# Flamingo block with two gated layers on one core: q and k of the second attention stacked in both halves of the partitions, its small matmuls as pairs of 64-row tiles

## What is computed

```python
def _L1_xattn_ref(query, key, value, Wq, Wk, Wv, Wo):   # DIM 512, 32 heads of 16, 8 key-value heads
    q = (query @ Wq).reshape(b, sq, 32, 16).transpose(0, 2, 1, 3)
    k = (key @ Wk).reshape(b, sk, 8, 16).transpose(0, 2, 1, 3)     # each serves 4 heads
    v = (value @ Wv).reshape(b, sk, 8, 16).transpose(0, 2, 1, 3)
    scores = jnp.einsum('bhqd,bhkd->bhqk', q, k) * 16 ** (-0.5)
    probs = jax.nn.softmax(scores, axis=-1)
    out = jnp.einsum('bhqk,bhkd->bhqd', probs, v)
    return out.transpose(0, 2, 1, 3).reshape(b, sq, DIM) @ Wo
x = x + jnp.tanh(g_xattn[1]) * _L1_xattn_ref(_layernorm(x), ctx_4096, ctx_4096, ...)
```

## Time and profile before

| | us |
|---|---|
| median of 3 runs | 1134.33 (1128.93 to 1134.96) |
| profiled execution, its own time | 1125.34 |
| its span, first to last instruction | 1123.5 |
| TensorE (PE) busy | 1012.8 |
| VectorE (DVE) busy | 665.8 |
| ScalarE (ACT) busy | 482.3 |
| GpSimd (POOL) busy | 376.5 |
| mean granted TensorE clock | 0.967 |

### The profile page before, as it was taken

The page is one execution under the profiler, slowest core; times in us unless marked ns, Lnnn a source line. Parts: engine busy times, 40 slices in busy tenths (PEclk is TensorE's granted clock), DMA queues, the critical chain, the costliest instruction groups (busy, mean ns, idle before and its releaser), DMA issues. The chain is left out here.

```text
span 1123.5 us, 18617 instructions
## 1 busy us (share of the span) xinstructions
PE 1012.8 (90%) x6780; PEld 877.3 (78%) x6780; DVE 665.8 (59%) x1128; ACT 482.3 (43%) x938; POOL 376.5 (34%) x251
## 2 busy tenths in 40 slices
PE   2989999999999999999999999998898579999964
PEld 1979889898898898989889898897776357777543
DVE  5467467457556646745745674673486546667396
ACT  2356336436535634643643563372131125555311
POOL 4306503711730640361173065032892300000054
PEclk9989999999999999999999999999998689999986
DMA  5001100100200110110020011000531173121000
GB/s 172 35 1 57 39 1 27 67 0 0 93 0 0 56 37 0 47 46 0 0 93 0 0 56 56 0 1 1 171 102 38 38 205 63 29 56 29 1 1 37
DMA packets 29617, 46.49 MB, mean 41 GB/s; under 512 B 3216, under 2 KB 12048, under 8 KB 29584
## 3 DMA queue, kind: packets, MB, share of 16 engines
q1 hardware_dynamic: 29008, 46.03, 13.5%
q10 hardware_dynamic: 576, 0.00, 0.0%
HBM read 41.83 MB, written 4.19 MB: 41 GB/s over the span
## 5 line engine op out<-in xcount | busy, mean ns | idle before, releaser
L446 DVE TENSOR_TENSOR ptL<-tbank,ptH 128x512 fp32r<-128x512 f32 x192 | 132.3, 689 | 84.5 <-ACT ptH L330 84.5
L330 ACT ACTIVATE ptH<-tbank 128x512 fp32r<-128x512 f32 x192 | 115.9, 604 | 109.2 <-PE tbank L554 108.9
L281 POOL TENSOR_TENSOR oTL<-o_norm,oTH 128x512 fp32r<-128x512 f32 x32 | 41.3, 1291 | 347.1 <-ACT oTH L350 347.1
L554 PE MATMUL tbank<-ident,probs 128*128 128x128 f32 x864 | 132.2, 276 | 16.6 <-DVE ptL L446 12.3
L459 DVE TENSOR_REDUCE negmax<-score 128x1 f32<-128x768 f32 x128 | 119.5, 949 | 19.5 <-PE score L74 19.5
L417 DVE TENSOR_REDUCE sumsq<-probs 128x2 f32<-128x256 f32 (+1 forms) x80 | 42.1, 526 | 142.3 <-ACT probs L325 71.8
L356 ACT ACTIVATE probs<-score,negmax 128x768 f32<-128x768 f32 x128 | 115.7, 904 | 15.4 <-DVE negmax L459 15.4
L72 PE MATMUL obank<-ptH,vH 128*128 128x256 f32 x384 | 121.8, 317 | 0.0
L554 PEld LDWEIGHTS tbank<-ident,probs 128*128 128x128 f32 x864 | 97.9, 140 | 26.9 <-DVE ptL L446 15.1
L276 POOL TENSOR_TENSOR rnorm<-sumsq,neg_half 128x2 f32<-128x2 f32 (+1 forms) x80 | 71.9, 901 | 111.3 <-DVE sumsq L419 111.3
L73 PE MATMUL score<-wkvL,kvT_hi 128*128 128x256 f32 x384 | 108.7, 283 | 0.0
(11 more groups left out here) (250 smaller groups left out, 2467.9 us busy)
## 6 DMA issues: line engine op xcount, KB each, us to landing
wqo_stage<-in_wq SPq DMA_DIRECT2D x9, 1024.0 KB, 5.7
wqo_stage<-in_wo SPq DMA_DIRECT2D x8, 1024.0 KB, 5.3
wkv_stage<-in_wkv SPq DMA_DIRECT2D x9, 512.0 KB, 6.5
a_qS<-q_scratch SPq DMA_DIRECT2D x32, 128.0 KB, 3.8
ctx_stage<-in_ctxT SPq DMA_DIRECT2D x2, 1024.0 KB, 14.0
kS<-k_scratch SPq DMA_DIRECT2D x32, 64.0 KB, 2.1
q_scratch<-part SPq DMA_DIRECT2D x8, 256.0 KB, 4.0
wqo_stage<-in_down_w SPq DMA_DIRECT2D x3, 512.0 KB, 4.8
```

The lines of the kernel that those rows point to most:

```text
L330: act.activation(out, tbank[c % 2][:], ACT.Copy, scale=scale).then_inc(t_hi, 1)
L446: i = dve.tensor_tensor(out, tbank[c % 2][:], f32(hi), ALU.subtract)
L554: i = pe.transpose(tbank[c % 2][:, n * P:(n + 1) * P], block_in, S.ident[:])
```

## The change

`qS` and `kS` hold the same 64-row stack twice, in partitions 0 to 63 and in 64 to 127, so `load_k` and `load_q` issue 8 DMAs each in place of 4 (`STACK` doubles with them), and both memsets to zero and the waits for them go. Every matmul of the scores pass, of the transposed scores and of the maxima takes 64 rows: of two neighbours one reads the low half and the other the high half, and they write different banks. The negative maxima of a unit are now 8 matmuls of 128 columns in two groups of four (`add_maxima`): in the first group (`begin_maxima`) the low rows add their 64 queries to bank 0 and the high rows theirs to bank 1, in the second (`finish_maxima`) the banks are exchanged. The second group is issued one turn later, behind `scores_T` of the next unit, and it is what now releases the exp (`pe_sT`). `negmax` has 4 buffers in place of 2. `times_v` moves to `v % 4 == 2`, the transposes to `v % 4 == 3`, and `finish_quad` to `v % 4 == 0` of the quad after that.

```diff
-            sp.wait_ge(k_zeroed, 1)
             for s in range(2):
                 S.load_k(sp, s, s)
...
-            pool.memset(f32(S.kS[64:P, :, :]), 0.0).then_inc(k_zeroed, 1)
-            pool.wait_ge(k_zeroed, 1)
...
-    negmax = sb("a_negmax", [P, 4], f32r)
+    MB = 4
+    negmax = sb("a_negmax", [P, 2 * MB], f32r)
...
-    STACK = 8 * 16
+    STACK = 16 * 16
+    H = P // 2
+    low, high = slice(0, H), slice(H, P)
...
-            sp.wait_ge(zeroed, 2)
-
             def load_q(g, s):
-                for n in range(4):
-                    heads = q_dram[n // 2].rearrange("(h d) n -> d h n", d=D1)
+                for n in range(8):
+                    heads = q_dram[n // 2 % 2].rearrange("(h d) n -> d h n", d=D1)
...
-            pool.memset(f32(qS[64:P, :, :, :]), 0.0).then_inc(zeroed, 1)
-            pool.wait_ge(zeroed, 2)
...
-                    if v % GRP == 3 and (not first or v >= GRP):
-                        finish_quad(i, r - 1, v // GRP - 1)
+                    if v % GRP == 0 and (not first or v >= 2 * GRP):
+                        finish_quad(i, r - 2, v // GRP - 2)
...
-            finish_quad(TURNS - 1, QUADS * TURNS - 1, QUADS - 1)
+            for w in (QUADS - 2, QUADS - 1):
+                finish_quad(TURNS - 1, QUADS * (TURNS - 1) + w, w)
...
-                    q = b * SQ + t * P
-                    pe.matmul(score[t][:], qS[:, s, j, q:q + P], kS[:, s, b * SC:(b + 1) * SC],
+                    q, rows = b * SQ + t * P, (low, high)[t]
+                    pe.matmul(score[t][:], qS[rows, s, j, q:q + P], kS[rows, s, b * SC:(b + 1) * SC],
                               start=True, stop=True).then_inc(pe_s, 1)
+
+            def add_maxima(v, order, stop):
+
+                for t in range(2):
+                    m = negmax[:, 2 * (v % MB) + t:2 * (v % MB) + t + 1]
+                    for half, rows in enumerate((low, high)):
+                        bank = scoreT[v % 2][:, 512 * order[half]:512 * (order[half] + 1)]
+                        q = t * P + H * half
+                        x = pe.matmul(bank.rearrange("p (k q) -> p k q", k=2)[:, :, q:q + H],
+                                      m[rows].to_broadcast([H, P]), ident_r[rows, rows].unsqueeze(1).to_broadcast([H, 2, H]),
+                                      start=False, stop=stop and t == 1)
+                return x
 
             def scores_T(n, v, first):
 
                 s, b, j = unit(v)
                 if not first or v >= 2:
                     pe.wait_ge(s_exp, n - 1)
+                for k in range(2):
+                    for half, rows in enumerate((low, high)):
+                        key = b * SC + (2 * half + k) * P
+                        pe.matmul(scoreT[v % 2][:, 512 * half + k * SQ:512 * half + (k + 1) * SQ], kS[rows, s, key:key + P],
+                                  qS[rows, s, j, b * SQ:(b + 1) * SQ], start=k == 0, stop=False)
+
+            def begin_maxima(n, v):
+
                 pe.wait_ge(s_max, 2 * n + 2)
...
-                x.then_inc(pe_sT, 1)
+                add_maxima(v, (0, 1), False).then_inc(pe_m, 1)
+
+            def finish_maxima(n, v):
+
+                pe.wait_ge(pe_m, n + 1)
+                add_maxima(v, (1, 0), True).then_inc(pe_sT, 1)
...
                     scores_T(n, v, first)
+                    if not first or v >= 1:
+                        finish_maxima(n - 1, (v - 1) % NU)
+                    begin_maxima(n, v)
                     if not first or v >= GRP:
-                        if v % GRP == 1:
+                        if v % GRP == 2:
                             times_v(r - 1, (v // GRP - 1) % QUADS, i if v >= GRP else i - 1, first)
-                        if v % GRP == 2:
+                        if v % GRP == 3:
                             transpose_o(r - 1, (v // GRP - 1) % 2)
...
             def load_k(sp, g, s):
 
-                for n in range(4):
+                for n in range(8):
```

More of the change, by code:

```diff
@@ L696, in ffn0 @@
     pe_v, v_done = sem("pe_v"), sem("v_rows_done")
-    k_zeroed, stats3_done = sem("k_zeroed"), sem("stats3_done")
+    stats3_done = sem("stats3_done")
     w_in = {n: sem(f"{n}_in") for n in ("gate", "affine")}
@@ L1251, in attn1 @@
     win = sem("a_win")
-    pe_s, s_max, ident_set = sem("a_pe_s"), sem("a_s_max"), sem("a_ident_set")
+    pe_s, pe_m, s_max, ident_set = sem("a_pe_s"), sem("a_pe_m"), sem("a_s_max"), sem("a_ident_set")
     pe_sT, s_exp, pe_pv = (sem(f"a_{n}") for n in ("pe_sT", "s_exp", "pe_pv"))
@@ L1375, in maxima @@
                     dve.wait_ge(pe_s, 2 * n + t + 1)
-                    dve.tensor_reduce(negmax[:, 2 * (v % 2) + t:2 * (v % 2) + t + 1], score[t][:], AX.X, ALU.max,
+                    dve.tensor_reduce(negmax[:, 2 * (v % MB) + t:2 * (v % MB) + t + 1], score[t][:], AX.X, ALU.max,
                                       negate=True).then_inc(s_max, 1)
@@ L1450, in scores_T @@
                     pe.wait_ge(s_exp, n - 1)
-                pe.wait_ge(s_max, 2 * n + 2)
[L1452 to L1461, removed]
-                x.then_inc(pe_sT, 1)
+                for k in range(2):
[4 more added lines that the diff above has]
+            def begin_maxima(n, v):
+                pe.wait_ge(s_max, 2 * n + 2)
+                add_maxima(v, (0, 1), False).then_inc(pe_m, 1)
+            def finish_maxima(n, v):
+                pe.wait_ge(pe_m, n + 1)
+                add_maxima(v, (1, 0), True).then_inc(pe_sT, 1)
             def times_v(r, w, i, first):
@@ L1500, in _ @@
             turns(pe, turn)
+            finish_maxima(NU * TURNS - 1, NU - 1)
             times_v(QUADS * TURNS - 1, QUADS - 1, TURNS - 1, False)
```

## The result

The changed kernel takes **1161.2 us** (median of 4 runs, 1152.43 to 1164.55), the kernel before beside it 1131.63 (4 runs, 1127.97 to 1134.96): ratio 1.0254, 95% interval 1.0202 to 1.0306. It is slower by 2.5%. The forecast, 1135 or no change, did not come. The time lies inside the range, but by luck: the range reached so far up only for rival 1, and the runs show another mechanism.

What follows compares the result with a forecast made beforehand. PE sets the pace, busy 137.9 of the loop's 142.5 us. Loop -3.7, memsets -3.0 and stack loads +7.3 sum to +0.6 on 1125.34, taken over to the median 1134.33: 1135 us, range 1124 to 1165.

Steps and rivals of the forecast that it cites:

- rival 1: In scores and maxima, the two halves' loads or matmuls run one after the other: +29, 1163 us; chance 0.25.
- The ring: Second attention, per unit: exp, transposed scores, second group of maxima, exp in series; 1.75 us, a quad 8.05 against 8.35.
- The long turn: Second attention, the turn that contains `times_v`, from exp to exp: 2.80 us.
- Pairs at the price of one: On PE, two 64-row matmuls running together cost what one does: 0.23 for four transposed scores, 0.22 per maxima group.
- The doubt that I had raised about weight loads: On PE, load time ignores row count; taken alone, a unit's 14 loads take 1.5 us and nothing would be won.
- The memset: Start of the second attention: without the 3.74 us memset into `qS`, DVE's normalization is not held up: -3.0 us.
- The stack loads: Start of the second attention: 16 DMAs in place of 8 delay the store of q tile 1: +7.3 us.
- The last interval: End of the loop, between the last two `times_v`: 4.6 us in place of 6.14, -1.5.
- rival 4: In the loop the granted clock falls to 1.2 GHz: quad near 12, 1190 us; chance 0.05 together with rival 5.
- rival 5: In the loop a slot's reload is late, beyond 2 us to spare: +6 at 3 us; chance 0.05 with rival 4.
- the first `times_v`: Start of the loop: it comes one unit later, +2.0 us, that is 1.75 and some 0.25 for the cold clock.
- The splits: Weight splits of the last turn lengthen exps about as much as they now stop DVE; surplus over 8.35 left unchanged.

Runs made afterwards that it cites:

- The run with the stacks alone: Kernel before with both memsets removed, both stacks loaded twice and q scaled by half, nothing in pairs: 1132.2 us, ratio 1.0028 to the kernel before.
- the whole rewrite with its four repairs: Changed kernel with DVE's splits two units later, `finish_maxima` before `scores_T`, slot 1's loads behind tile 2, `times_v` in halves: 1123.63 us, ratio 0.9936.

## What the prediction had right and wrong, step by step

- **The ring** stands as described: PE waits for the exp ahead of L1463, the exp for L1450. Its size was a little off: 8.38 a quad where I had 8.05. The long turn is 2.92 by the exps above (2.80 predicted), the others 1.79 to 1.87 (1.75). Mis-sized are the transposed scores behind a wait, 0.34 where I had 0.23, and the two scores behind `times_v`, 0.33 (965.42 to 965.75) where I had 0.24; from the maxima to the exp it was 0.37 where I had 0.45. The loop therefore gained next to nothing at full clock (-1.2), where I had -4.2.
- **Pairs at the price of one** held: 0.24 for four transposed scores in a dense row (0.23), and 0.17 for a group of four maxima (0.22 taken, between my 0.11 and 0.44). The two scores of a unit are a pair only behind `times_v`; in the other turns the second waits for DVE's maxima and starts some 0.55 later (970.59 against 970.04), under the exp. Rival 1 is refuted, though the time came out at its 1163: right number, wrong mechanism, and luck for the range. The doubt that I had raised about weight loads falls with it: the loads of the two halves overlap. The Trainium skill says this of row tiles as well (TensorE: Matmul & The Clock Gate, Packing small matmuls: a weight load for other rows is pulled ahead of matmuls in flight), and had I weighed it, rival 1 would have had less than 0.25.
- **The memset**: -3.0 predicted. The four normalizations now take 2.05 us in a row, and from the identity's copy at 885.52 to PE's projection at 890.93 it is 5.4, before 8.3: -2.9. Right. But the memset had a second effect that I did not price: PE's clock, 0.50 before the projection in both kernels, is back at about 891 in the changed one and at about 896 before, and from the projection's start to the store of tile 0 it is 5.1 us in place of 6.9: -1.8. The run with the stacks alone, without the memset too, has 5.1 as well.
- **The stack loads**: ACT's wait for the store is 14.76 us (near 14 predicted); first scores 918.27, +4.4 against +4.3. The agreement is luck in part: from the store of tile 0 to the first scores it is +8.0 (22.3 against 14.3) where I had +7.3, the projection gave back 1.8, and 1.1 is the later start of the phase. Without that the start cost +3.3.
- **The last interval**, 4.6: measured 4.63. Right. No reload is late in the changed kernel: right, with the reload 13.7 long and not 12.
- **The clock (rival 4, given a chance of 0.05 together with rival 5)** is the first failed step: "over a stretch with PE busy 0.73 of 3 us the granted clock was 1.00 [...]; the loop will be far busier". Busy share by the profile was the wrong measure: PE shows 0.92 busy over 20 us at a clock of 0.50, and 0.95 or more in the quads in which the clock falls. A unit's matmuls have as many columns as before (3072), but half the rows, in the same time; that this is the cause is not shown, only that the clock follows what PE does in the loop. The price was about +9.4 in six quads and 2 to 4 of the +3.9 ahead of the first `times_v` (+2.0 predicted, most of it the unit more): between 11 and 13 of the 27 us, without its part in the splits, and not the 55 of a loop that is cold throughout.
- **The splits** are the second: "lengthen exps in the ring about as much as they now stop DVE, so I leave the average's surplus". Cost +11.9. I had priced ACT's 0.6 us and not followed the wait: DVE's `split_lo` waits for an ACT instruction that stands behind an exp that has moved a turn later.

So of the 26.3 us between forecast and balance (26.9 against +0.6) the splits are 11.9, the clock in six quads 9.4, the ring's size over the loop 3.0 (-1.2 against -4.2) and the first `times_v` 1.9; the other terms come to 0.1, with the misses at the start that cancel.

## What to carry to other kernels

Halving the work of the busiest engine gives nothing if the new order ties the engines into a ring that is as long; write the ring down, open it, and then look for the next bound (here DVE behind `times_v`, then the doubled reloads), each of which took back much of what the last edit gave. When an instruction's release moves a turn later, follow every instruction that stands behind it on its engine into its waiters on the other engines, rare stages included. And before a large rewrite try the one-line edit on the old kernel: moving one load behind a store gave 0.3%, with an interval that overlaps that of the whole rewrite with its four repairs.

## What the hardware showed that I had not expected

- With pairs of 64-row matmuls the granted clock stays at 0.50 for 20.2 us with PE shown busy 18.67 of them, and over 21.3 after a short idle stretch, where full matmuls bring it to 1.00 in 6.4; and it falls again in some quads at full speed. In the changed kernel every rise in the loop comes in `times_v`, 32 matmuls of 128 rows in a row, or right behind it. More matmuls, though useless, keep it up, and so does an order in which the same matmuls don't stand in a ring. What exactly in the two kinds of work makes the difference is open: the traces don't separate the rows used, the columns and the gaps.
- Eight paired matmuls of 128 columns start 0.041 us apart, each with its own weights, where single full ones start 0.11 apart.
- Each change between 128-row and 64-row matmuls costs 0.2 us (0.43 between starts where 0.235 was before).
- In one trace each, 1.86 us of PE idle time left the clock at 1.00 and 5.4 us did not.
